# Perceiver mixer on one core: keys projected by weight columns of four strips and dealt on chip to stacked rows

## The chip, the core and the metric

One core of a Trainium2 chip runs the whole program in one launch. The metric is device time in microseconds from a timed run; lower is better. The kernel before was timed three times; a profiled execution was taken besides.

## What is computed

One block of a perceiver over 32 batches of 64 tokens of width 256: cross attention to 1601 context tokens per batch (16 heads of 16), a selective scan, and a mixture of 64 experts with top 8, each behind a layer norm and added to x. The change concerns the attention scores:

```python
q = _qdq(x) @ _qdq(wq).T + bq
kv = cond @ wkv.T + bkv
k, v = jnp.split(kv, 2, axis=-1)
...
attn = jax.nn.softmax(jnp.einsum('bnhd,bmhd->bhnm', q, k) * scale, axis=-1)
o = jnp.einsum('bhnm,bmhd->bnhd', attn, v).reshape(B, N, C)
```

## The kernel before

There are three phases: the mixer (attention, scan, routing), the experts, and a combining phase. The change touches the mixer alone. It works on 16 pairs of batches. A pair has 16 strips, called slots 0 to 15 of the pair: a strip is one batch, two heads by 64 queries (128 rows), against all 1604 padded keys. `step_of` (L371) turns a strip's number into batch `b`, half of the width `g` and place `s` among four. The 1604 keys lie in four chunks (`QUADS`) of 401 (`CK`).

Every engine runs the same loop over strips G. In TensorE's loop (L748) a strip does, in order: scores of G (`scores`, L616); transposes of the probabilities of strip G-1 (`turn`, L633), in two parts; one unit of the values of a coming batch (`v_mm`, L606; none in slots 0 and 8); the other transposes; the product of probabilities and values for four strips in flight (`times_v`, L643); keys for strip G+4 (`k_mm`, L594). Between them stand the small jobs of the table `MIX` (L58): the query product, output transposes, projections and routing of other pairs; slot 5 has `oqT` and `proj`, slot 8 has `XQ` ahead of the keys and `Q` behind them.

The keys of one strip are 32 rows wide. `k_mm` multiplies 32 weight columns by the four chunks and puts chunk c on PSUM partitions 32c to 32c+31, so four products of 32 columns stand side by side in TensorE. ScalarE (`k_up`, L780) writes the rounded high part `K_hi` from PSUM with the bias, VectorE (`k_low`, L959) the remainder `K_lo`; both are in the reduced fp32r format. `scores` then forms hi x hi, hi x lo and lo x hi, each as four products of 32 rows in the four row tiles, added up in the four banks of `S`. The queries are split the same way on GpSimd (`part_q`, L489) and copied by SP (`deal_queries`, L394) to all four groups of 32 partitions, eight transfers per half pair.

PSUM has one tile `S` of four banks, a ring of three banks for keys, values, transposes and small jobs in the order of the list `JOBS` (L131), and `O`. A job takes the bank of the job three places earlier when ScalarE (transposes) or VectorE (all others) has freed it (`take`, L559). VectorE takes the maximum of S over 1604 columns (`strip_max`, L976), ScalarE the exponential (`soft`, L796).

SP issues all transfers but the scatters, in the program order of its own loop (L418): query deals in slots 0 and 12, one zeroing transfer per strip in the first 48 strips (`clear`, `clear_y`), x rows, the next contexts in slots 4 and 11 (`load_ctx`), and, in slot 6 of a pair with a mixer turn, the row matrix B and C out to memory and, after waiting for it, back as `BC` to all partitions (L441 to L447).

## Time and profile before

| | us |
|---|---|
| timed runs, median of three (lowest, highest) | 2299.77 (2297.57, 2302.56) |
| profiled execution, first to last instruction (span) | 2296.0 |
| TensorE (PE) busy | 2102.5 (92%) |
| VectorE (DVE) busy | 1751.3 (76%) |
| ScalarE (ACT) busy | 1441.0 (63%) |
| GpSimd (POOL) busy | 684.0 (30%) |

The record of the profiled execution has its span; what lies around the span is seen only in the timed runs, whose median is 3.8 us longer. TensorE's products are pipelined: each record lasts longer than the step from one to the next, so the work of a block is read from the start of one block to the start of the next, not from busy time. A line of the time listing merges neighbouring records of one line and shape; a record count of twice the products means fp32, which takes two passes. A line of busy time by stretch holds the window, its us, a comma, the busy us (and records) of PE, PEld, DVE, ACT and POOL, then the granted clock (PEclk), the mean busy share of the 16 DMA engines, which may pass 1 by overlap at the edges, and GB/s.

### The profile page before, as it was taken

Reading aid. Unit: us, or ns where it says so; the run is one execution under the profiler, and the core shown is the slowest. Engines: PE = TensorE matmul, PEld = TensorE weight load, DVE = VectorE, ACT = ScalarE, POOL = GpSimd, SP = SyncE. Lnnn points to the kernel's source line nnn. Section 1 sums busy time; section 2 is a strip of 40 time slices with the busy share of each in tenths; the row PEclk is TensorE's granted clock in tenths of the full one; section 3 lists DMA queues with packets and bytes.
Section 4 is the critical chain, followed back from the end, with each engine's and each line's share of the span. In section 5 each row is a group of like instructions: output and inputs, shape, how many; then the busy total and the mean of one; then the engine's idle time right before and its main releaser. Section 6 shows DMA issues by size and latency. Waiting matters only on the chain. (4 is left out here: it accounts for less than half of the span.)

```text
span 2296.0 us, 56054 instructions
## 1 busy us (share of the span) xinstructions
PE 2102.5 (92%) x21448; PEld 1456.2 (63%) x21448; DVE 1751.3 (76%) x3728; ACT 1441.0 (63%) x3012; POOL 684.0 (30%) x646
## 2 busy tenths in 40 slices
PE   7999999999999999999999999999997149999975
PEld 5666666666666666666666666666664037777754
DVE  5557887979797978888888888797978736656646
ACT  2667676768676767676777767676867124444433
POOL 1002040404131322213130404040403427767770
PEclk9999999999999999999999999999999569999998
DMA  7586672323132313232323323232310136676648
GB/s 226 192 288 210 235 250 75 114 82 89 72 89 72 93 70 91 77 83 79 100 88 82 97 64 105 55 105 68 107 47 25 56 119 212 199 229 209 201 138 331
DMA packets 132711, 294.16 MB, mean 128 GB/s; under 512 B 21899, under 2 KB 89143, under 8 KB 126304
## 3 DMA queue, kind: packets, MB, share of 16 engines
q1 hardware_dynamic: 114016, 255.89, 35.7%
q0 software_dynamic: 18432, 34.69, 4.3%
q8 instruction: 174, 2.85, 0.5%
q14 instruction: 89, 0.73, 0.1%
HBM read 165.40 MB, written 108.27 MB: 119 GB/s over the span
## 5 line engine op out<-in xcount | busy, mean ns | idle before, releaser
L801 ACT ACTIVATE sb_probs<-S,sb_negmax 128x1604 f32<-128x1604 f32 x256 | 409.2, 1598 | 278.5 <-DVE sb_negmax L979 277.0
L793 ACT ACTIVATE sb_probsT<-W 128x384 f32<-128x384 f32 (+1 forms) x1024 | 473.6, 513 | 68.2 <-PE W L639 65.3
L639 PE MATMUL W<-sb_ident,sb_probs 128*128 128x128 f32 (+1 forms) x3328 | 478.3, 280 | 15.7 <-DVE sb_o_tok L992 8.0
L979 DVE TENSOR_REDUCE sb_negmax<-S 128x1 f32<-128x1604 f32 x256 | 466.2, 1821 | 2.9 <-PE S L629 1.2
L639 PEld LDWEIGHTS W<-sb_ident,sb_probs 128*128 128x128 f32 (+1 forms) x3328 | 363.5, 139 | 133.9 <-issue 64.7
L612 PE MATMUL W<-sb_wkv_in,sb_ctx 128*128 128x256 f32 (+1 forms) x1664 | 410.7, 389 | 14.2 <-ACT sb_probsT L793 6.6
L602 PE MATMUL W<-sb_ctx,sb_wkv_in 128*32 128x401 f32 x4096 | 399.3, 504 | 4.4 <-DVE sb_V L973 2.9
L612 PEld LDWEIGHTS W<-sb_wkv_in,sb_ctx 128*128 128x128 f32 (+1 forms) x1664 | 293.3, 187 | 79.1 <-ACT sb_probsT L793 25.7
L1335 POOL DMA_INDIRECT y_scratch<-sb_ys,sb_places x256 | 264.4, 1033 | 112.1 <-issue 109.0
L963 DVE SCALAR_TENSOR_TENSOR sb_K_lo<-W,sb_pair_cols,sb_K_hi 128x401 fp32r<-128x401 f32 x256 | 162.2, 633 | 175.5 <-ACT sb_K_hi L785 175.2
L785 ACT ACTIVATE sb_K_hi<-W,sb_pair_cols 128x401 fp32r<-128x401 f32 x256 | 153.2, 598 | 181.5 <-PE W L602 181.4
L512 POOL TENSOR_TENSOR sb_bx<-sb_u,sb_BC 128x512 f32<-128x512 f32 x128 | 164.9, 1305 | 340.9 <-DVE sb_u L1105 219.3
L657 PE MATMUL O<-sb_probsT,sb_V 128*32 128x128 f32 (+1 forms) x6656 | 245.0, 277 | 0.0
L602 PEld LDWEIGHTS W<-sb_ctx,sb_wkv_in 128*32 128x32 f32 x4096 | 129.2, 110 | 120.5 <-issue 104.1
L657 PEld LDWEIGHTS O<-sb_probsT,sb_V 128*32 128x32 f32 (+1 forms) x6656 | 173.9, 110 | 48.1 <-issue 39.5
L524 POOL DMA_INDIRECT xe_scratch<-sb_row,sb_sc_idx x128 | 156.2, 1221 | 43.8 <-issue 31.0
L973 DVE COPY sb_V<-W 128x512 f32<-128x512 f32 (+1 forms) x224 | 144.9, 647 | 26.1 <-PE W L612 25.1
L629 PEld LDWEIGHTS S<-sb_K_hi,sb_Q_hi 32*128 32x128 f32 x1024 | 49.8, 182 | 161.4 <-issue 158.9
L540 POOL TENSOR_TENSOR sb_st<-sb_st,sb_neg_half 128x1 f32<-128x1 f32 x16 | 8.8, 548 | 422.7 <-DVE sb_st L1086 422.7
L1456 DVE TENSOR_TENSOR sb_hid<-U,sb_sg 96x512 f32<-96x512 f32 x64 | 44.0, 687 | 112.5 <-PE U L1364 111.6
L535 POOL TENSOR_TENSOR sb_st<-sb_st,sb_neg_half 128x1 f32<-128x1 f32 x16 | 9.1, 566 | 397.3 <-DVE sb_st L893 397.3
L629 PE MATMUL S<-sb_K_hi,sb_Q_hi 32*128 32x400 f32 (+1 forms) x1024 | 116.5, 444 | 11.4 <-ACT sb_probs L801 9.3
(188 smaller groups left out, 2921.0 us busy)
## 6 DMA issues: line engine op xcount, KB each, us to landing
sb_ctx<-ctxT SPq DMA_DIRECT2D x32, 1604.0 KB, 7.7
xe_scratch<-sb_none SPq DMA_DIRECT2D x32, 1088.0 KB, 12.7
sb_xg<-xe_scratch SPq DMA_DIRECT2D x64, 544.0 KB
sb_BC<-bc_scratch SPq DMA_DIRECT2D x32, 1024.0 KB, 5.9
sb_Q_hi<-sb_q_hi SPq DMA_DIRECT2D x128, 128.0 KB, 4.5
sb_Q_lo<-sb_q_lo SPq DMA_DIRECT2D x128, 128.0 KB, 5.4
y_scratch<-sb_none SPq DMA_DIRECT2D x16, 1024.0 KB, 12.0
sb_rows<-y_scratch SPq DMA_DIRECT2D x16, 1024.0 KB, 8.1
```

The source lines that it names most:

```text
L512: pool.tensor_tensor(bx[:, mine, :], u[:, h, :].unsqueeze(1).to_broadcast([P, QS, P]), BC[:, mine, :], ALU.mult).then_inc(pool_up, 1)
L524: pool.indirect_dma_start(dram["xe"], bass.IndirectOffsetOnAxis(ap=sc_idx[:, t:t + 1], axis=0), row3[:], None, bounds_check=E * CAP - 1, o ...
L602: ins = pe.matmul(W[32 * c:32 * c + 32, 0:CK], wkv_in[:, k, w0:w0 + 32], ctx_t[b][:, k, c * CK:(c + 1) * CK], start=(k == 0), stop=(k == D ...
L612: ins = pe.matmul(W[0:keys_in(t), n * D:(n + 1) * D], ctx_t[b][:, k, t * P:t * P + keys_in(t)], wkv_in[:, k, D:2 * D], start=(k == 0), sto ...
L629: ins = pe.matmul(S[:, 512 * c:512 * c + cn], q[half][rows, s, g, :, :].rearrange("p h n -> p (h n)"), k[rows, s, 0:cn], start=(n == 0), s ...
L639: ins = pe.transpose(W[0:keys_in(t), at * P:(at + 1) * P], probs[n % 2][:, t * P:t * P + keys_in(t)], ident[:])
L657: ins = pe.matmul(O[32 * s:32 * s + 32, 0:P], V[b][0:keys_in(t), t, g * P + 32 * s:g * P + 32 * s + 32], probsT[k][n % (k + 1)][0:keys_in( ...
L793: act.activation(probsT[k][n % (k + 1)][:, 0:wide], ring[bank_of("T", G, k)][:, 0:wide], ACT.Copy)\
L801: act.activation(probs[n % 2][:].rearrange("p (c k) -> p c k", c=QUADS), scores_of, ACT.Exp, bias=negmax[:, slot:slot + 1], accum_out=den[ ...
L963: dve.scalar_tensor_tensor(K_lo[:, s, 0:CK], bank("K", n)[:, 0:CK], pair_cols[:, g * STRIPS + s:g * STRIPS + s + 1], K_hi[:, s, 0:CK].bitc ...
L979: dve.tensor_reduce(negmax[:, slot:slot + 1], scores_of, AX.XY, ALU.max, negate=True).then_inc(max_done, 1)
L1335: pool.indirect_dma_start(dram["y"], bass.IndirectOffsetOnAxis(ap=places[e % 4][:, c:c + 1], axis=0), ys[n][:, c, :], None, bounds_check=T ...
```

## The change

The weight columns of four strips (a full 128) are multiplied by one chunk at a time, so one key job now gives chunk c for four strips, and four jobs give all chunks. `K_hi` and `K_lo` hold 128 rows (four strips by 32) and are doubled. SP deals each strip's 32 rows to a tile `K_of` as hi, lo, hi on rows 0 to 95 (three transfers per strip, `deal_keys`), and the queries to `Q_of` as hi, hi, lo. Scores are then one product of 96 rows for each chunk. Key jobs run six strips ahead (`LEAD`), not four; the zeroing transfers are spread over more strips. The bias is a column per half, not per strip.

```diff
+CLEAR_AT = {n + n // 4: n for n in range(CLEARS)}
+Y_CLEAR_AT = {48 + 4 * n: n for n in range(Y_CLEARS)}
...
+
+LEAD = 6
...
     turns = [("T", G, k) for k in range(STRIPS)] if 0 < G <= ALL_STRIPS else []
...
-    keys = [("K", G + STRIPS)] if G + STRIPS < ALL_STRIPS else []
+    keys = [("K", G + LEAD)] if G + LEAD < ALL_STRIPS else []
...
-START = [("K", 0), ("K", 1), ("XQ", 0), ("K", 2), ("Q", 0), ("K", 3)]
+START = [("K", 0), ("K", 1), ("XQ", 0), ("K", 2), ("Q", 0), ("K", 3), ("K", 4), ("K", 5)]
...
         + [job for G in range(END) for job in jobs_at(G)])
...
-        K_hi, K_lo = (sb(f"K_{m}", [P, STRIPS, CK + 1], F32R) for m in ("hi", "lo"))
+        K_hi, K_lo = ([sb(f"K_{m}{n}", [P, QUADS, CK + 1], F32R) for n in range(2)] for m in ("hi", "lo"))
+        K_of = [sb(f"K_of{n}", [P, QUADS, CK + 1], F32R) for n in range(2)]
...
-        Q_hi, Q_lo = ([sb(f"Q_{m}{n}", [P, STRIPS, 2, 2, N], F32R) for n in range(2)] for m in ("hi", "lo"))
+        Q_of = [sb(f"Q_of{n}", [P, STRIPS, 2, 2, N], F32R) for n in range(2)]
...
         probsT = [[sb(f"probsT{k}{n}", [P, WIDTHS[0] * P]) for n in range(k + 1)] for k in range(STRIPS)]
...
+        k_in = [sem(f"k_in{n}") for n in range(2)]
...
-            (q_cols[:], io["bq"]), (pair_cols[:], io["bk"]),
+            (q_cols[:], io["bq"]), (k_cols[:], io["bk"]),
...
                 sp.wait_ge(q_up, pair + 1)
                 after(sp, s_done, pair * SLOTS - SLOTS // 2 * (1 - half))
-                for part, whole in ((q_hi, Q_hi), (q_lo, Q_lo)):
-                    for c in range(QUADS):
-                        sp.dma_start(whole[half][32 * c:32 * c + 32, :, :, :, :].rearrange("p s g h n -> p s (g h n)").bitcast(F32),
-                                     part[:, 2 * half:2 * half + 2, :, :].rearrange("p g h n -> p (g h n)").bitcast(F32)).then_inc(q_in[half], 16)
+                for at, part in enumerate((q_hi, q_hi, q_lo)):
+                    sp.dma_start(Q_of[half][32 * at:32 * at + 32, :, :, :, :].rearrange("p s g h n -> p s (g h n)").bitcast(F32),
+                                 part[:, 2 * half:2 * half + 2, :, :].rearrange("p g h n -> p (g h n)").bitcast(F32)).then_inc(q_in[half], 16)
+
+            def deal_keys(n):
+
+                four, s = divmod(n, STRIPS)
+                sp.wait_ge(ring_free["dve"], free_at("K", four * QUADS + QUADS - 1))
+                after(sp, s_done, n - 1)
+                for at, part in enumerate((K_hi, K_lo, K_hi)):
+                    sp.dma_start(K_of[n % 2][32 * at:32 * at + 32, :, :].rearrange("p c k -> p (c k)").bitcast(F32),
+                                 part[four % 2][32 * s:32 * s + 32, :, :].rearrange("p c k -> p (c k)").bitcast(F32)).then_inc(k_in[n % 2], 16)
             def clear(n):
...
             deal_queries(0, 0)
+            deal_keys(0)
+            deal_keys(1)
             sp.wait_ge(none_up, 1)
             for G in range(END):
...
+                if G + 2 < ALL_STRIPS:
+                    deal_keys(G + 2)
                 if slot == 0 and cur:
                     deal_queries(i, 1)
                 if slot == 12 and nxt:
                     deal_queries(i + 1, 0)
-                if G < CLEARS:
-                    clear(G)
-                elif G < CLEARS + Y_CLEARS:
-                    clear_y(G - CLEARS)
+                if G in CLEAR_AT:
+                    clear(CLEAR_AT[G])
+                if G in Y_CLEAR_AT:
+                    clear_y(Y_CLEAR_AT[G])
                 if slot == 0 and nxt:
                     sp.wait_ge(ring_full, full_at("XQ", i))
...
                     after(sp, dve_up, dve_at(i - 2, "X2"))
...
                 if nxt and slot in (4, 11):
-                    sp.wait_ge(ring_full, full_at("K", G + STRIPS - (1 if slot == 4 else 0)))
+                    sp.wait_ge(ring_full, full_at("K", i * SLOTS + (7 if slot == 4 else 15)))
                     load_ctx(i + 1, slot // 8)
                 if m == 2 and p is not None:
                     sp.wait_ge(ring_free["dve"], free_at("xp", p))
...
-            for part in (K_hi, K_lo):
+            for part in (*K_hi, *K_lo):
...
-                    after(pool, q_in[half], 16 * 2 * QUADS * i)
+                    after(pool, q_in[half], 16 * 3 * i)
...
             def k_mm(n):
-                b, g, s = step_of(n)
+                b, g, c = step_of(n)
                 W = take("K", n)
                 pe.wait_ge(ctx_in[b], 16 * (n // SLOTS + 1))
-                w0 = g * P + 32 * s
                 for k in range(DT):
-                    for c in range(QUADS):
-                        ins = pe.matmul(W[32 * c:32 * c + 32, 0:CK], wkv_in[:, k, w0:w0 + 32],
-                                        ctx_t[b][:, k, c * CK:(c + 1) * CK], start=(k == 0), stop=(k == DT - 1))
+                    ins = pe.matmul(W[:, 0:CK], wkv_in[:, k, g * P:(g + 1) * P],
+                                    ctx_t[b][:, k, c * CK:(c + 1) * CK], start=(k == 0), stop=(k == DT - 1))
...
             def v_mm(pair, b, unit):
...
                 if s == 0 and g == 0:
-                    pe.wait_ge(q_in[half], 16 * 2 * QUADS * (n // SLOTS + 1))
-                pe.wait_ge(ring_free["dve"], free_at("K", n))
+                    pe.wait_ge(q_in[half], 16 * 3 * (n // SLOTS + 1))
+                pe.wait_ge(k_in[n % 2], 16 * 3 * (n // 2 + 1))
                 after(pe, exp_done, n)
-                products = ((Q_hi, K_hi), (Q_hi, K_lo), (Q_lo, K_hi))
-                for n, (q, k) in enumerate(products):
-                    for c in range(QUADS):
-                        rows = slice(32 * c, 32 * c + 32)
-                        cn = CK + 1 if c == 0 else CK - 1
-                        ins = pe.matmul(S[:, 512 * c:512 * c + cn], q[half][rows, s, g, :, :].rearrange("p h n -> p (h n)"),
-                                        k[rows, s, 0:cn], start=(n == 0), stop=(n == len(products) - 1))
+                for c in range(QUADS):
+                    cn = CK + 1 if c == 0 else CK - 1
+                    ins = pe.matmul(S[:, 512 * c:512 * c + cn], Q_of[half][0:96, s, g, :, :].rearrange("p h n -> p (h n)"),
+                                    K_of[n % 2][0:96, c, 0:cn], start=True, stop=True)
                 ins.then_inc(s_done, 1)
             def turn(G, k):
...
-                if G + STRIPS < ALL_STRIPS:
-                    k_mm(G + STRIPS)
+                if G + LEAD < ALL_STRIPS:
+                    k_mm(G + LEAD)
...
             def k_up(n):
-                _, g, s = step_of(n)
+                _, g, c = step_of(n)
+                four = n // QUADS
                 act.wait_ge(ring_full, full_at("K", n))
-                after(act, s_done, n - STRIPS + 1)
-                act.activation(K_hi[:, s, 0:CK], ring[bank_of("K", n)][:, 0:CK], ACT.Identity,
-                               bias=pair_cols[:, g * STRIPS + s:g * STRIPS + s + 1]).then_inc(k_hi_up, 1)
+                if c == 0:
+                    for half in range(2):
+                        after(act, k_in[half], 16 * 3 * 2 * (four - 1))
+                act.activation(K_hi[four % 2][:, c, 0:CK], ring[bank_of("K", n)][:, 0:CK], ACT.Identity,
+                               bias=k_cols[:, g:g + 1]).then_inc(k_hi_up, 1)
             def turned(G, k):
...
-            for n in range(STRIPS):
+            for n in range(LEAD):
...
-                if G + STRIPS < ALL_STRIPS:
-                    k_up(G + STRIPS)
+                if G + LEAD < ALL_STRIPS:
+                    k_up(G + LEAD)
...
             def k_low(n):
-                _, g, s = step_of(n)
+                _, g, c = step_of(n)
+                four = n // QUADS
                 dve.wait_ge(k_hi_up, n + 1)
-                dve.scalar_tensor_tensor(K_lo[:, s, 0:CK], bank("K", n)[:, 0:CK],
-                                         pair_cols[:, g * STRIPS + s:g * STRIPS + s + 1],
-                                         K_hi[:, s, 0:CK].bitcast(F32), ALU.add, ALU.subtract).then_inc(ring_free["dve"], 1)
+                dve.scalar_tensor_tensor(K_lo[four % 2][:, c, 0:CK], bank("K", n)[:, 0:CK], k_cols[:, g:g + 1],
+                                         K_hi[four % 2][:, c, 0:CK].bitcast(F32), ALU.add, ALU.subtract).then_inc(ring_free["dve"], 1)
             def v_up(pair, b, unit):
...
                 if slot == 6 and i >= 2:
...
-                if G + STRIPS < ALL_STRIPS:
-                    k_low(G + STRIPS)
+                if G + LEAD < ALL_STRIPS:
+                    k_low(G + LEAD)
                 if slot == 8 and nxt:
...
     def cols(v):
...
-    def pair_cols(v):
-        return np.tile(v.reshape(DT * STRIPS, 2 * DH).T, (QUADS, 1))
-
...
-        "bk": pair_cols(a["L0_xattn_bkv"][:D]), "bv": a["L0_xattn_bkv"][D:],
+        "bk": cols(a["L0_xattn_bkv"][:D]), "bv": a["L0_xattn_bkv"][D:],
```

## Rows read from the trace of the kernel before

**Rows 1.** Busy time by stretch, the mixer's; columns as told above.
```profile
33.00:1760.00 1727.00, 1671.95 (x19226) 1132.68 (x19230) 1408.74 (x2889) 1223.32 (x2559) 378.84 (x335) 1.00 0.35 110
```

**Rows 2.** Busy time by stretch, three strips: slots 5, 13 and 15.
```profile
932.07:940.39 8.32, 7.84 (x83) 5.33 (x79) 5.91 (x14) 4.17 (x8) 0.55 (x1) 1.00 0.01 2
...
987.38:994.26 6.88, 6.45 (x78) 4.45 (x74) 6.32 (x11) 5.36 (x13) 1.65 (x2) 1.00 0.95 199
...
1000.87:1007.09 6.22, 6.22 (x78) 4.44 (x74) 5.73 (x9) 5.44 (x12) 0.00 (x0) 1.00 0.48 107
```

**Rows 3.** PE in order of time, slot 15: start, us, engine, line, operation.
```profile
1000.87 0.45 PE L629 MATMUL S<-sb_K_hi,sb_Q_hi 32*128 32x402 f32 x4
1001.15 0.35 PE L629 MATMUL S<-sb_K_lo,sb_Q_hi 32*128 32x402 f32 x4
1001.34 0.35 PE L629 MATMUL S<-sb_K_hi,sb_Q_lo 32*128 32x402 f32 x4
1001.62 0.98 PE L639 MATMUL W<-sb_ident,sb_probs 128*128 128x128 f32 x7
1002.44 1.92 PE L612 MATMUL W<-sb_wkv_in,sb_ctx 128*128 128x256 f32 x8
1004.20 0.82 PE L639 MATMUL W<-sb_ident,sb_probs 128*128 128x128 f32 x6
1004.95 0.86 PE L657 MATMUL O<-sb_probsT,sb_V 128*32 128x128 f32 x24
1005.62 1.53 PE L602 MATMUL W<-sb_ctx,sb_wkv_in 128*32 128x401 f32 x16
1007.09 0.46 PE L629 MATMUL S<-sb_K_hi,sb_Q_hi 32*128 32x402 f32 x4
```

**Rows 4.** PE in order of time, slot 8 from probabilities times values on.
```profile
956.75 1.08 PE L657 MATMUL O<-sb_probsT,sb_V 128*32 128x128 f32 x32
957.76 0.44 PE L581 MATMUL W<-sb_ident,sb_x_q 128*128 128x128 f32 x2
...
959.61 1.16 PE L590 MATMUL W<-sb_xqT,sb_wqT 128*128 128x128 f32 x8
960.70 0.45 PE L629 MATMUL S<-sb_K_hi,sb_Q_hi 32*128 32x402 f32 x4
```

**Rows 5.** PE and DVE in order of time in the experts' phase, one expert.
```profile
1998.86 1.04 PE L1353 MATMUL XT<-sb_ident,sb_xg 128*128 128x128 f32 x8
...
1999.73 1.89 PE L1375 MATMUL Y<-sb_wd,sb_hid 96*128 96x256 f32 x8
2000.13 1.28 DVE L1430 TENSOR_TENSOR sb_x_lo<-XT,sb_x_hi 128x512 fp32r<-128x512 f32 x2
...
2001.52 0.68 PE L1364 MATMUL G<-sb_x_hi,sb_w_hi 128*96 128x512 f32 x2
```

**Rows 6.** PE and DVE in order of time, slot 5 and the start of slot 6.
```profile
937.19 1.13 PE L685 MATMUL W<-sb_wpT,sb_oqT 128*128 128x256 f32 x4 [0.48 <-DVE sb_V L973]
...
938.25 0.86 PE L657 MATMUL O<-sb_probsT,sb_V 128*32 128x128 f32 x24
...
941.17 0.64 DVE L963 SCALAR_TENSOR_TENSOR sb_K_lo<-W,sb_pair_cols,sb_K_hi 128x401 fp32r<-128x401 f32 x1 [0.34 <-ACT sb_K_hi L785]
```

**Rows 7.** Busy time by stretch: query deals, deals crowded, BC, early, later.
```profile
1003.00:1004.00 1.00, 1.00 (x7) 0.87 (x6) 1.00 (x1) 1.00 (x3) 0.00 (x0) 1.00 0.71 237
...
988.00:990.00 2.00, 1.57 (x17) 1.16 (x10) 1.93 (x5) 2.00 (x8) 1.09 (x1) 1.00 1.16 190
950.00:954.00 4.00, 4.00 (x53) 2.71 (x51) 3.45 (x8) 3.15 (x6) 0.00 (x0) 1.00 1.02 422
33.00:140.00 107.00, 103.35 (x1192) 71.37 (x1192) 53.50 (x69) 69.23 (x127) 3.88 (x4) 0.98 0.69 240
...
900.00:1000.00 100.00, 97.07 (x1118) 65.84 (x1121) 83.53 (x181) 70.06 (x147) 26.17 (x23) 1.00 0.26 81
```

**Rows 8.** SP's queue in order of time: the two BC loads of one pair.
```profile
948.28 0.81 SPq L446 DMA_DIRECT2D sb_BC<-bc_scratch  x2
```

More of the change, by code:

```diff
@@ L230, in mixer_phase @@
         q_cols = sb("q_cols", [P, DT])
-        pair_cols = sb("pair_cols", [P, DT * STRIPS])
+        k_cols = sb("k_cols", [P, DT])
         bv_row = sb("bv_row", [P, D])
@@ L470, in _ @@
                       allow_small_or_imprecise_dtypes=True).then_inc(consts, 1)
-            pool.wait_ge(consts, 9)
+            pool.wait_ge(consts, 11)
             pool.affine_select(out=ident[:], in_=ident[:], compare_op=ALU.not_equal, fill=1.0, base=0,
@@ L478, in _ @@
                                pattern=[[1, P]], channel_multiplier=-1).then_inc(consts, 1)
-            pool.wait_ge(consts, 12)
+            pool.wait_ge(consts, 14)
             pool.affine_select(out=headmask[:], in_=headmask[:], compare_op=ALU.is_ge, fill=0.0, base=DH * STRIPS - 1,
                                pattern=[[DH * STRIPS, 2]], channel_multiplier=-1).then_inc(consts, 1)
-            pool.wait_ge(consts, 13)
+            pool.wait_ge(consts, 15)
             def rstd_q(i):
@@ L564, in take @@
                 return ring[bank_of(*job)]
-            pe.wait_ge(consts, 13)
+            pe.wait_ge(consts, 15)
             def turn_w(rows, bank, parts):
```

## Prediction

> **What bounds the kernel now.** I read the stretches first, then the strips of one pair, then TensorE's blocks inside a strip, then the places where TensorE waits, then the DMA share. The mixer takes 1727 us of the 2296.0 us span; PE is busy 1672 us of it at granted clock 1.00, the 2.4 GHz level [rows 1]. Every step of the diff lies in this stretch. 256 strips in 1727 us are 6.75 us each. A strip with no extra work (slot 15 of a pair) takes 6.22 us, all PE [rows 2], and its blocks add up to that with nothing over: scores 0.75, seven transposes 0.82, values 1.76, six transposes 0.75, probs times values 0.67, keys 1.47 [rows 3]. So there PE's own time is the strip. Not everywhere: slot 13 has the same jobs and takes 6.88, and slot 5 takes 8.32 [rows 2], where proj adds 1.06 [rows 6] and oqT, two transposes and the way into the next block, some 0.4: 7.7. The rest is waiting on a bank that VectorE has not freed. In slot 5 proj waits for the copy of V, and K_lo then waits for K_hi, made from this strip's keys [rows 6]: a loop through both engines. By the same subtraction slots 1 to 6, 10, 13 and 14 hold 0.5 us or more of waiting; 0, 7, 9, 11, 12 and 15 are PE's; 8 is discussed below. So a price on PE must be taken apart by where in the strip it falls.
>
> **Keys.** Before: eight products of 32 weight columns per strip, four at a time in the four column tiles. After: two products of 128 columns per strip, each two passes of 401 columns. The values block is such work: 8 passes of 256 columns in 1.76 us are 0.22 each [rows 3], so 401 columns are 0.34, and four passes 1.35 or so. The old block is 1.47, that is also four rounds of 0.34, plus 0.02 of stagger and about 0.09 until the scores may start. The column tiles were already full; full weight columns gain nothing by themselves.
>
> **Scores.** Before: three products (hi hi, hi lo, lo hi), each four row tiles at once, a steady step of 0.19 (1001.15 to 1001.34; both ends are rounded, I use 0.18) [rows 3]. After: one product over 96 rows, four chunks one after another: four passes, not three, 4 x 0.18 = 0.73. So the stacking adds a pass of 0.18.
>
> **Changes of tile shape.** What can pay for that pass is what PE loses each time the tile shape changes. Leaving row tiles: the last step is 0.28, not 0.19, and the seven transposes take 0.82, which is 0.06 over 7 x 0.109 (0.109 is the step of the eight in [rows 5]). Entering them: the first step is 0.28, 0.10 over the steady one, after the 0.09 at the end of keys [rows 3]. Together 0.34 per strip, gone if 96 rows run as the full array. They seem to: eight 128-row transposes take 0.87, 8 x 0.109 with nothing added, though the next products have 96 rows; the 0.06 at their other end comes with a VectorE result that ended at 2001.41, 0.1 before PE went on, so it is a wait [rows 5]. But a new change appears, from probs times values (column tiles, unchanged) to full-width keys, which used to share the shape. Its price is in slot 8: 32 records of probs times values take 1.01 before a full transpose, against 0.67 x 32/24 = 0.89, so 0.12; and the eight passes of the query product, between column tiles and row tiles, take 1.09 where steps of 0.11 give 0.89; 0.09 of the rest is the exit, 0.10 a first weight load that could not run ahead [rows 4]. Entry to full-width keys: 0.22.
>
> The Trainium skill, "TensorEngine Tiling (Array Packing)", Key Properties, says that a change of tiling mode drains the engine, and its list of modes has 128, 64 and 32 rows, none of 96. By it the 96 rows either cost nothing or, if they were a mode, would keep the drains; the rows here show no price.
>
> **Sum for a strip that is PE's own**, from the end of probs times values to the second transpose. Before: 1.47 + 0.75 + 0.06 = 2.28. After: 0.22 + 1.35 + 0.73 = 2.30. Net +0.02 (bounds: -0.20 if the entry price stays hidden, +0.13 if the change from plain fp32 products to fp32r ones costs 0.11, as [rows 5] could also be read: 0.06 ahead of the first and as much in a first weight load that did not run ahead).
>
> **Strips with a loop through VectorE.** There the 0.34 saved lies around the scores, where PE waits for a bank anyway, while the 0.22 lies ahead of keys, in the loop keys, K_hi, K_lo, maximum, V copy. So from 0 (VectorE alone sets the pace) to +0.22 (the loop of slot 5 [rows 6]); slot 13 waits without an added PE block, so neither end holds for all nine, and I take +0.11.
>
> **Slot 8** runs XQ ahead of keys and Q behind them, both full: two changes fewer there, 0.5 us less PE, but VectorE is busy with routing; I count -0.2 (0 to -0.5).
>
> Per pair: six at +0.02, slot 8 at -0.2, nine at +0.11: +0.9 us; 16 pairs +14 us (bounds -5 and +34).
>
> **ScalarE and VectorE.** k_up and k_low keep count, shape and place; only the bias column differs. k_up's new wait, once per four strips, is for deals issued two strips before: free. LEAD 6 puts two key blocks (2.9 us of PE) into the start and takes them from the last strips; at the start PE waits for VectorE, so I take 0 (bounds -3 to +3). Four memsets instead of two on POOL run during the weight loads: nothing.
>
> **Deals.** New: per strip three transfers of 32 x 6432 bytes, 617 KB. No such transfer is in the trace; the nearest is the query deal, also onto 32 partitions: 237 GB/s when it starts, 190 GB/s at full DMA share with several in flight [rows 7]. So 2.6 to 3.3 us per strip of 6.75; I take 3. Query deals fall from 16 to 6 per pair and give back about 7 us per pair. Later in the mixer the share is 0.26 [rows 7]: 26 + 45 - 7 = 64 of 109 us, no bound. Early, with the clears, it is 0.69 of 107 us [rows 7]: 74 + 42 to 53 - 7 - 8 (three clears fewer in 16 strips) = 101 to 112 of 107. That can just saturate: 0 to 5 us per pair for two and a half pairs, I take 4 us in all (bounds 0 to 20).
>
> The Trainium skill, "SBUF — State Buffer", Door 1, speaks against this part: 32 partitions reach 8 of 16 ports, 189 GB/s at 1 MiB, and two transfers do not add up; estimate by it 3.3 us per strip, the slow end of the rows.
>
> SP now waits in every strip for the scores two strips ahead of use, and all that it issues later queues behind that: contexts, BC, x. A deal issued after the scores of G must land before those of G+2, 12 to 14 us later; issue is about 2 us and transfer 3. The tightest is slot 9's: BC's 2 MB are issued at 948.28 [rows 8], move at 422 GB/s [rows 7], are through near 954, the deal takes till about 957 and lands near 959; the scores were at 960.70 [rows 4]. One us to spare: hidden, but barely.
>
> **Forecast.** 2296.0 + 14 + 4 = 2314 us of span. The median of the runs, 2299.77, lies 3.8 above the profiled span; so 2318 us.
>
> **Rivals.**
> *The entry to full-width keys is hidden* (faster). The weight load of the first key pass runs ahead under probs times values. For: ordinary full-to-full changes cost 0. Against: [rows 4] price it after the same block. Then -0.20 in six strips, about -0.1 in nine, slot 8 -0.3: -2.4 per pair, -38 us, half of it eaten by VectorE's loops: about 2283. It decides as soon as the measured entry is under about 0.1 us.
> *All is absorbed* (same). The mixed strips take 0 and the early DMA holds: 2296 + 2 + 0 to 4, 2303 on the median.
> *The scores pay at their entry* (slower). 0.11 in each strip, +27 us, less a third absorbed: 2336.
> *Deals land late* (slower). If BC and the deal together need 3 us more than reckoned, slot 9 is 2 us late per pair, +32 us: 2350. It shows as PE waiting for a DMA at the scores.
> *No full columns in effect*: the products are what the diff says, so I give this nothing.
>
> **Chances.** Forecast (2308 to 2328) 0.42; hidden entry 0.16; absorbed 0.18; scores pay 0.13; late deals 0.11. The range 2292 to 2350 leaves out the hidden entry and the far end of late deals. A measurement of this kernel can tell about 0.2% (2295.2 to 2304.4) from no change: faster 0.16, within 0.20, slower 0.64.
>
> **What would show it.** Keys start to scores start near 1.45, scores start to first transpose near 0.73, probs times values 0.12 longer: right. Scores with a first step well over 0.18: 96 rows do pay. Key blocks without a longer first pass: hidden entry. PE idle at the scores with a DMA as releaser: late deals. DMA share of 33 to 250 us at 0.95 or more with longer strips only there: the clears collide. The prediction is wrong if the strip of slot 15 moves by more than 0.1 us either way, or if the strips with waiting do not grow.

## Result and the profile after

The kernel after takes 2323.22 us (median of four runs, 2321.43 to 2324.79), the kernel before on the same chip 2298.96 (2297.57 to 2302.56): ratio 1.0104, 95% interval 1.0092 to 1.0116. It is slower by 1.0%, as forecast (2318, range 2292 to 2350). The sum of the span, by stretches between the first scores of the pairs in TensorE's time listing:

| stretch | before, us | after, us | forecast | measured |
|---|---|---|---|---|
| start to the first scores | 33.40 | 37.21 | 0 | +3.8 |
| pairs 0 to 2 | 317.19 | 327.84 | +2.7 and +4 | +10.65 |
| pairs 3 to 14 | 1313.05 | 1324.71 | +10.8 | +11.66 |
| pair 15, to its last scores | 96.13 | 93.67 | +0.9 | -2.5 |
| behind that | 536.2 | 538.5 | 0 | +2.3 |
| span | 2296.0 | 2321.9 | +18.4 | +25.9 |

Three lines of the page of after: PE's busy time, DMA shares in 40 slices, and SP's queue (packets, MB, share of 16 engines). The transfers went from 294.16 to 430.68 MB in all.
```profile
PE 2119.4 (91%) x16328; PEld 1593.0 (69%) x16328; DVE 1752.0 (75%) x3728; ACT 1444.9 (62%) x3012; POOL 677.4 (29%) x648
...
DMA  6999976767677766566666657565745136666648
...
q1 hardware_dynamic: 127840, 393.02, 61.5%
```
Busy time by stretch of after, columns as in [rows 1]: the mixer; slots 5, 13 and 15 of pair 8, answering [rows 2]; pair 1 and pair 2 with the clears, then a later stretch, answering [rows 7].
```profile
37.20:1784.05 1746.85, 1683.33 (x14153) 1264.38 (x14154) 1408.19 (x2886) 1226.23 (x2559) 369.15 (x335) 1.00 0.70 187
...
951.48:959.95 8.47, 7.88 (x62) 5.86 (x60) 6.08 (x14) 4.17 (x8) 0.36 (x1) 1.00 0.64 208
1007.47:1014.35 6.88, 6.49 (x55) 4.98 (x54) 6.36 (x10) 5.62 (x14) 1.86 (x2) 1.00 0.81 201
1020.96:1027.30 6.34, 6.34 (x55) 4.95 (x54) 5.79 (x9) 5.44 (x12) 0.00 (x0) 1.00 0.46 99
...
140.69:250.04 109.35, 105.11 (x893) 79.39 (x891) 79.90 (x138) 76.98 (x160) 14.45 (x13) 1.00 0.94 285
250.04:365.05 115.01, 108.62 (x902) 81.66 (x901) 92.64 (x195) 78.11 (x164) 25.38 (x23) 0.99 0.78 220
...
900.00:1000.00 100.00, 96.91 (x825) 72.57 (x824) 82.52 (x180) 68.72 (x142) 18.64 (x19) 1.00 0.60 149
```
Slot 15 went from 6.22 to 6.34, slot 5 from 8.32 to 8.47, slot 13 stayed at 6.88; the DMA share is 0.94 in pair 1 and 0.60 later (0.26 before). PE in order of time in slot 15, answering [rows 3] (start, us, line, operation):
```profile
1020.96 1.20 PE L642 MATMUL S<-sb_K_of,sb_Q_of 96*128 96x402 f32 x4
1021.99 0.93 PE L652 MATMUL W<-sb_ident,sb_probs 128*128 128x128 f32 x7
1022.79 1.99 PE L628 MATMUL W<-sb_wkv_in,sb_ctx 128*128 128x256 f32 x8
1024.62 0.82 PE L652 MATMUL W<-sb_ident,sb_probs 128*128 128x128 f32 x6
1025.37 0.87 PE L670 MATMUL O<-sb_probsT,sb_V 128*32 128x128 f32 x24
1026.16 1.61 PE L618 MATMUL W<-sb_ctx,sb_wkv_in 128*128 128x401 f32 x4
1027.30 0.66 PE L642 MATMUL S<-sb_K_of,sb_Q_of 96*128 96x402 f32 x1
```
From start to start: scores 1.03, transposes 0.80, values 1.83, transposes 0.75, probs times values 0.79, keys 1.14. The scores' first record now begins while the last key pass still runs, so keys and scores are read together: 2.17. Of the entry to full-width keys, 0.12 shows as the longer block ahead of them (0.79 against 0.67), 0.10 as the first key pass (0.44; the others take 0.34).

A steady pair (the sum of the medians over pairs 2 to 14, slot by slot) takes 110.37 us against 109.35: +1.01. Single slots go from -0.24 (slot 1) and -0.20 (slot 4) to +0.21 (slot 0) and +0.34 (slot 3); slots 11, 13 and 14 stand still.

### The profile page after: what moved, and what is told of

It is laid out like the page before. It is cut to its first block and busy times, and to the rows that moved or that the text cites. A ratio compares the mean times of both kernels' runs of the same rounds, so it can differ in the third digit from the quotient of the medians.

```text
span 2321.9 us, 46485 instructions
## 1 busy us (share of the span) xinstructions
PE 2119.4 (91%) x16328; PEld 1593.0 (69%) x16328; DVE 1752.0 (75%) x3728; ACT 1444.9 (62%) x3012; POOL 677.4 (29%) x648
## 2 busy tenths in 40 slices
DMA packets 146500, 430.68 MB, mean 185 GB/s; under 512 B 31627, under 2 KB 78391, under 8 KB 140128
## 5 line engine op out<-in xcount | busy, mean ns | idle before, releaser
L652 PE MATMUL W<-sb_ident,sb_probs 128*128 128x128 f32 (+1 forms) x3328 | 466.4, 276 | 17.2 <-DVE sb_o_tok L1008 5.9
L652 PEld LDWEIGHTS W<-sb_ident,sb_probs 128*128 128x128 f32 (+1 forms) x3328 | 385.6, 139 | 79.4 <-DVE sb_o_tok L1008 16.7
L618 PE MATMUL W<-sb_ctx,sb_wkv_in 128*128 128x401 f32 x1024 | 413.4, 527 | 4.8 <-DVE sb_V L989 2.6
L642 PE MATMUL S<-sb_K_of,sb_Q_of 96*128 96x400 f32 (+1 forms) x1024 | 296.8, 412 | 16.3 <-ACT sb_probs L817 9.4
L980 DVE SCALAR_TENSOR_TENSOR sb_K_lo<-W,sb_k_cols,sb_K_hi 128x401 fp32r<-128x401 f32 x256 | 162.1, 633 | 194.4 <-ACT sb_K_hi L801 193.9
L801 ACT ACTIVATE sb_K_hi<-W,sb_k_cols 128x401 fp32r<-128x401 f32 x256 | 152.9, 597 | 208.4 <-PE W L618 205.1
L618 PEld LDWEIGHTS W<-sb_ctx,sb_wkv_in 128*128 128x128 f32 x1024 | 175.0, 190 | 129.7 <-issue 39.8
L642 PEld LDWEIGHTS S<-sb_K_of,sb_Q_of 96*128 96x128 f32 x1024 | 188.6, 191 | 85.8 <-issue 23.7
L542 POOL DMA_INDIRECT xe_scratch<-sb_row,sb_sc_idx x128 | 147.7, 1154 | 43.9 <-issue 31.1
```

Source lines behind the costliest of these rows:

```text
L618: ins = pe.matmul(W[:, 0:CK], wkv_in[:, k, g * P:(g + 1) * P], ctx_t[b][:, k, c * CK:(c + 1) * CK], start=(k == 0), stop=(k == DT - 1))
L642: ins = pe.matmul(S[:, 512 * c:512 * c + cn], Q_of[half][0:96, s, g, :, :].rearrange("p h n -> p (h n)"), K_of[n % 2][0:96, c, 0:cn], star ...
L652: ins = pe.transpose(W[0:keys_in(t), at * P:(at + 1) * P], probs[n % 2][:, t * P:t * P + keys_in(t)], ident[:])
L801: act.activation(K_hi[four % 2][:, c, 0:CK], ring[bank_of("K", n)][:, 0:CK], ACT.Identity, bias=k_cols[:, g:g + 1]).then_inc(k_hi_up, 1)
L980: dve.scalar_tensor_tensor(K_lo[four % 2][:, c, 0:CK], bank("K", n)[:, 0:CK], k_cols[:, g:g + 1], K_hi[four % 2][:, c, 0:CK].bitcast(F32), ...
```

## The two parts taken apart

The first three kernels are the kernel before with the keys alone, the scores alone, or both, and no transfers. Without the deals the scores multiply rows that are not the right ones; the work has the same shapes.

**Keys alone**, in the kernel before:
```diff
-                    for c in range(QUADS):
-                        ins = pe.matmul(W[32 * c:32 * c + 32, 0:CK], wkv_in[:, k, w0:w0 + 32],
-                                        ctx_t[b][:, k, c * CK:(c + 1) * CK], start=(k == 0), stop=(k == DT - 1))
+                    ins = pe.matmul(W[:, 0:CK], wkv_in[:, k, g * P:(g + 1) * P],
+                                    ctx_t[b][:, k, s * CK:(s + 1) * CK], start=(k == 0), stop=(k == DT - 1))
```


> The kernel before with one part of the change: keys by full weight columns (two products of 128 columns), everything else as before. It leaves out the dealing, so the rows of K hold other strips' keys and the scores are of the wrong keys. Theory (tile changes set the price): a new change of shape ahead of the keys, none gone around the scores; slot 15 of a pair goes from 6.22 to about 6.42 us, first key pass 0.44 with later ones 0.34, all runs near 2340 (2325 to 2350). Rival (full columns are cheaper by themselves, or the entry is hidden): slot 15 at or under 6.22, 2300 or less. Rival (the slowdown of the whole change comes from the transfers): no change, 2299.

Measured: 2323.18 us (2321.10 to 2323.69), ratio 1.0103 (1.0086 to 1.0120); slot 15 takes 6.39, a steady pair 110.7. PE in order of time, from probs times values of slot 15 to the scores:
```profile
1016.83 0.87 PE L655 MATMUL O<-sb_probsT,sb_V 128*32 128x128 f32 x24
1017.62 1.61 PE L600 MATMUL W<-sb_ctx,sb_wkv_in 128*128 128x401 f32 x4
1019.17 0.46 PE L627 MATMUL S<-sb_K_hi,sb_Q_hi 32*128 32x402 f32 x4
```
Keys take 1.55 to the scores and probs times values 0.79: 2.34, where [rows 3] has 0.67 + 1.47 = 2.14. The full columns cost 0.20 here and gain nothing; 0.03 of it is given back at the values, which no longer wait. 25 us in all, about as much as the whole change; the time lies 2 us under its range (2325 to 2350).

**Scores alone**, in the kernel before:
```diff
-                products = ((Q_hi, K_hi), (Q_hi, K_lo), (Q_lo, K_hi))
...
+                for c in range(QUADS):
+                    cn = CK + 1 if c == 0 else CK - 1
+                    ins = pe.matmul(S[:, 512 * c:512 * c + cn], Q_hi[half][0:96, s, g, :, :].rearrange("p h n -> p (h n)"),
+                                    K_hi[0:96, s, 0:cn], start=True, stop=True)
```


> The kernel before with the other part: scores as one product of 96 rows in four chunks, keys in column tiles as before. It leaves out the dealing and the low parts, so the products are taken of rows that lie there. Theory: a pass more (+0.18), no drain behind the scores (-0.14): slot 15 at 6.24 to 6.28, all runs 2298 to 2312. Rival (stacking saves time by itself): 2285 or less. Rival (an entry price for 96 rows of its own, 0.1 or more): slot 15 at 6.35 or more, 2320 or more.

Measured: 2299.23 us (2296.40 to 2302.30), ratio 1.0005 (0.9996 to 1.0015); slot 15 takes 6.22, a steady pair 109.3. PE in order of time, slot 15:
```profile
1000.63 1.00 PE L626 MATMUL S<-sb_K_hi,sb_Q_hi 96*128 96x402 f32 x4
1001.46 0.93 PE L636 MATMUL W<-sb_ident,sb_probs 128*128 128x128 f32 x7
1002.23 1.89 PE L612 MATMUL W<-sb_wkv_in,sb_ctx 128*128 128x256 f32 x8
```
Scores 0.83 for 0.75, transposes 0.77 for 0.82, values 1.72 for 1.76: four passes over 96 rows cost what three products in four row tiles and their way out cost.

**Both, no transfers**: the two edits together.

> Both parts together on the kernel before, without the transfers of keys and with keys four strips ahead as before; scores are of the wrong rows. Theory: here the change of shape between keys and scores goes too, so it is not the sum of the two parts: slot 15 at 6.35 as in the changed kernel, early pairs without their extra 7 us and the start without its 3.8: 2312 (2307 to 2317). Rival (transfers cause the slowdown): 2299 or less. Rival (parts add up): over 2340.

Measured: 2315.28 us (2314.66 to 2318.95), ratio 1.0070 (1.0053 to 1.0087); slot 15 takes 6.35, a steady pair 110.4. So the stacked product gives back 8 of the 25 us that full-width keys cost, the rest of the slowdown without transfers is +17 us, and the last 8 come with the transfers, the longer lead and the respread clears; the lead was not run by itself.

## The wait that the sum of slot 15 missed

PE's own sum was +0.02 for slot 15, the trace shows +0.13. In after the values block starts only when VectorE has made `K_lo` and so freed its bank. ScalarE and VectorE in order of time, slot 15 of before, then of after:
```profile
1001.01 0.60 ACT L785 ACTIVATE sb_K_hi<-W,sb_pair_cols 128x401 fp32r<-128x401 f32 x1 [0.80 <-PE W L602]
...
1001.68 0.63 DVE L963 SCALAR_TENSOR_TENSOR sb_K_lo<-W,sb_pair_cols,sb_K_hi 128x401 fp32r<-128x401 f32 x1
```
```profile
1021.47 0.60 ACT L801 ACTIVATE sb_K_hi<-W,sb_k_cols 128x401 fp32r<-128x401 f32 x1 [0.96 <-PE W L618]
...
1022.10 0.64 DVE L980 SCALAR_TENSOR_TENSOR sb_K_lo<-W,sb_k_cols,sb_K_hi 128x401 fp32r<-128x401 f32 x1
```
`K_lo` ends at 1002.31 in before and at 1022.74 in after. The first pass of the values takes 0.249 and 0.320 us, so the second starts at 1002.69 and 1023.11, in both 0.37 to 0.38 behind the end of `K_lo`: both wait for it, before by 0.03 (a pass is 0.218), after by 0.10, with another 0.03 in the last of the transposes. What changed is PE's way there: from `K_hi`'s start to the values 1.43 us in before, 1.32 in after. Not only the nine strips with a visible loop, this one too had no time to spare.

**Bank freed by ScalarE**, in the kernel after: `K_hi`'s completion frees the bank, and VectorE makes `K_lo` from SBUF.
```diff
-    return "act" if job[0] == "T" else "dve"
+    return "act" if job[0] in ("T", "K") else "dve"
...
-                               bias=k_cols[:, g:g + 1]).then_inc(k_hi_up, 1)
+                               bias=k_cols[:, g:g + 1]).then_inc(ring_free["act"], 1)
...
-                dve.scalar_tensor_tensor(K_lo[four % 2][:, c, 0:CK], bank("K", n)[:, 0:CK], k_cols[:, g:g + 1],
+                dve.scalar_tensor_tensor(K_lo[four % 2][:, c, 0:CK], K_hi[four % 2][:, c, 0:CK].bitcast(F32), k_cols[:, g:g + 1],
```


> The changed kernel with the PSUM bank of the keys freed by ScalarE as soon as K_hi is written; K_lo is computed by VectorE from K_hi in SBUF with the same size, so the low part is left out of the result. Theory (what the changed kernel saves around the scores it gives back at the values block, which waits for the bank that K_lo frees): the values block starts without its wait, slot 15 goes from 6.35 to about 6.25, and the whole by 10 to 25 us, to 2298 to 2313. Rival (the longer strip comes from TensorE's own steps alone): slot 15 stays at 6.35 and the whole within 5 us of 2323.

Measured: 2316.46 us (2314.99 to 2319.12), ratio 1.0074 (1.0057 to 1.0091). PE in order of time, slot 15:
```profile
1015.84 1.20 PE L643 MATMUL S<-sb_K_of,sb_Q_of 96*128 96x402 f32 x4
1016.87 0.93 PE L653 MATMUL W<-sb_ident,sb_probs 128*128 128x128 f32 x7
1017.64 1.89 PE L629 MATMUL W<-sb_wkv_in,sb_ctx 128*128 128x256 f32 x8
1019.37 0.82 PE L653 MATMUL W<-sb_ident,sb_probs 128*128 128x128 f32 x6
```
Transposes 0.77, values 1.73: the wait is gone and slot 15 takes 6.21. The time missed its range (2298 to 2313): the steady pair fell by 0.16 us only, since slot 13 gained 0.73 (6.88 to 6.15) and slot 14 lost 0.48 (6.61 to 7.09), and slot 9 lost as much (6.42 to 6.90).

**The same in the kernel before**:

> The kernel before, with the keys' bank freed by ScalarE after K_hi; VectorE makes K_lo from K_hi in SBUF, so the low part is not the true remainder. Theory (the values block waits for K_lo only in the kernel after, because its keys and scores are together 0.04 us shorter than the work of ScalarE and VectorE beside them): slot 15 can lose only the 0.03 us by which its first pass of values (0.249) is over 0.218, so 6.19; the pair loses 0 to 0.4 us, 2293 to 2299 us in all. Rival (the wait lies in every kernel alike and moving the bank is a gain of its own): slot 15 loses 0.13 us as it did in the kernel after, 6.09, and the time is 2292 us or less.

Measured: 2297.01 us (2295.83 to 2302.76), ratio 0.9992 (0.9983 to 1.0001); slot 15 takes 6.20, a steady pair 109.31. The theory's numbers. PE in order of time, slot 15:
```profile
1002.18 0.99 PE L639 MATMUL W<-sb_ident,sb_probs 128*128 128x128 f32 x7
1003.00 1.89 PE L612 MATMUL W<-sb_wkv_in,sb_ctx 128*128 128x256 f32 x8
1004.73 0.82 PE L639 MATMUL W<-sb_ident,sb_probs 128*128 128x128 f32 x6
```
The values take 1.73 here too. Where neither kernel waits for `K_lo`, slot 15 is 6.20 and 6.21: PE's own net is +0.01 where the sum had +0.02, and 0.11 is the wait. In the pair this wait is the smaller part. With the bank freed by ScalarE in both kernels a steady pair still differs by 0.90 us (110.21 against 109.31): slots 7, 12 and 15 then stand at +0.05, 0.00 and +0.01, but slot 0 keeps its +0.20, and slots 2, 3, 5, 6 and 10 keep +0.12 to +0.34.

**No low part**, in both: `K_lo` is filled with zeros once and VectorE's step left out.

> The kernel before without VectorE's part of the keys: K_lo is zero for good, the bank is freed by ScalarE, the products stay as they are. To be read against the next one. Theory (what the change adds to a steady pair goes through K_lo, the bank that it frees and VectorE; PE's own sum is level, 6.22 against 6.21): without K_lo the steady pairs of the two kernels differ by at most 0.3 us, and this one takes 2230 to 2285 us. Rival (PE's entry to full-width keys is paid in the strips with a loop whatever VectorE does): the pairs still differ by 0.9 us or more.

> The kernel after without VectorE's part of the keys: K_lo is zero for good, the bank is freed by ScalarE, the transfers stay, the clears are moved out of strips 20 to 24. Theory: a steady pair within 0.3 us of that of the kernel before without K_lo, and the time within 5 us of it (the start is 3 to 4 us longer and the last pair as much shorter). Rival: the pair is longer by 0.9 us or more and the time by 14 us or more.

Measured: 2231.87 us (2229.33 to 2233.67) and 2255.01 (2251.64 to 2262.99), each against 2300.33 of before on that chip: ratios 0.9705 (0.9692 to 0.9718) and 0.9818 (0.9801 to 0.9835). The steady pairs are 105.02 and 105.71: +0.70, more than the theory's 0.3, less than the rival's 0.9. So, by subtraction, 0.32 of the 1.01 us goes through VectorE's `K_lo`, and 0.70 does not. That part lies in slots 0, 10 and 14 (+0.15 to +0.16 each) and 6 (+0.10); nine strips, slot 15 among them, stand at +0.02 to +0.04; slots 3, 4 and 9 at +0.23, -0.20 and -0.18. PE in order of time in slot 14, scores and the values, of the first kernel and then of the second:
```profile
750.04 0.45 PE L628 MATMUL S<-sb_K_hi,sb_Q_hi 32*128 32x402 f32 x4
...
752.22 1.08 PE L611 MATMUL W<-sb_wkv_in,sb_ctx 128*68 128x256 f32 x4 [0.45 <-ACT sb_probsT L792]
```
```profile
760.17 1.20 PE L645 MATMUL S<-sb_K_of,sb_Q_of 96*128 96x402 f32 x4
...
762.71 1.08 PE L631 MATMUL W<-sb_wkv_in,sb_ctx 128*68 128x256 f32 x4 [0.57 <-ACT sb_probsT L812]
```
In slot 14 it is the same thing with another engine: the values wait for a bank that ScalarE frees, 0.57 us instead of 0.45. That what is saved around the scores (0.34 us less the added pass of 0.18) goes into this wait, which is 0.12 longer, while the 0.22 paid ahead of the keys stays, is what the two records suggest; no run takes ScalarE's copies away, and for slots 0, 3, 6 and 10 the cause is open. The medians of the runs differ by 23 us, not by 16 times 0.70: in the second kernel pairs 0 to 2 take 314.6 us against 307.7, and PE waits for dealt keys in later pairs too (slot 8 of pair 11: 8.40 against 6.53). With strips 0.3 us shorter some of the deals no longer land in time.

## Where the keys stand in the strip

**Keys ahead of probs times values**, in the kernel after and in the kernel before. Keys then follow transposes, which are full-width too.
```diff
-                    if in_flight(G):
-                        times_v(G)
...
-                    if in_flight(G):
-                        times_v(G)
                 if G + LEAD < ALL_STRIPS:
                     k_mm(G + LEAD)
+                if in_flight(G):
+                    times_v(G)
```


> The changed kernel with the keys block moved ahead of probabilities times values in each strip; same work, same result. The number of changes of shape stays. Theory (loops through VectorE run over the keys, and the values block waits for K_lo): K_lo comes 0.7 us earlier, the wait at the values block goes, strips that wait on VectorE get shorter; against it keys wait for the bank that the copy of V frees, 0.2 us in ordinary strips. 2290 to 2312. Rival (the wait for the bank of V takes all of it): 2320 or more.

> The kernel before with the same move alone. Theory: the loops through VectorE get shorter by up to 0.5 us in the nine slots that wait: 2265 to 2295. Rival: keys wait for the bank of V: 2300 or more.

Measured: 2331.93 us (2330.50 to 2355.58), ratio 1.0176 (1.0121 to 1.0231), and 2295.45 (2292.34 to 2298.94), ratio 0.9986 (0.9977 to 0.9996): the rival's time in the first, just over the theory's range in the second. PE in order of time, slot 15 of the first:
```profile
1026.59 0.82 PE L652 MATMUL W<-sb_ident,sb_probs 128*128 128x128 f32 x6
1027.54 1.61 PE L618 MATMUL W<-sb_ctx,sb_wkv_in 128*128 128x401 f32 x4
1029.08 0.86 PE L670 MATMUL O<-sb_probsT,sb_V 128*32 128x128 f32 x24
1029.88 0.45 PE L642 MATMUL S<-sb_K_of,sb_Q_of 96*128 96x402 f32 x1
```
The transposes take 0.95 until the keys instead of 0.75: keys now wait for VectorE's copy of V, which frees their bank. And the price of the changed shape has only moved: keys 1.54, probs times values 0.80, and the scores' first pass 0.29. One block in column tiles costs one way in and one way out in both places. In before the move gained 0.60 in slot 13 and 0.53 in slot 2, lost 0.65 in slot 1 and 0.20 in slot 15, and the pair fell by 0.37 (109.35 to 108.98): the one kernel that leaves out no work and whose interval lies below before's time, by 0.14%.

**The same in slots 12 and 13 alone**, of the kernel before:

> The kernel before, with the block of keys ahead of probs times values in slots 12 and 13 of every pair only. Theory (the order pays where the transposes or proj behind it wait for K_lo, and costs 0.2 us where keys then wait for the copy of V; with it everywhere, slots 13 and 14 lost 0.60 and 0.09 us, slot 12 gained 0.08): slot 13 at 6.28 instead of 6.88, slots 14 and 15 at 6.5 to 6.6 and 6.22, the steady pair 108.7 to 108.9, 2288 to 2293 us. Rival (VectorE's sequence sets the pace here, and what slot 13 gains is handed back in slots 14 and 15, as it was with the bank freed by ScalarE): the pair stays at 109.2 to 109.4, 2296 to 2301 us.

Measured: 2300.60 us (2296.08 to 2304.02), ratio 1.0005 (0.9996 to 1.0014), a steady pair 109.41, the rival's numbers: slot 13 fell to 6.28 as expected, but slot 12 rose from 6.56 to 7.31, for the keys stood there 0.67 us for the copy of V. PE's record of it:
```profile
766.50 1.55 PE L603 MATMUL W<-sb_ctx,sb_wkv_in 128*32 128x401 f32 x16 [0.67 <-DVE sb_V L976]
```
What one strip gains here a neighbour loses, but not the neighbours that the rival named: slots 14 and 15 take 6.52 and 6.22, and the loss lies in slot 12, in the wait that the theory had put at 0.2 us.

## The transfers

One strip's deal in after, a time without other loads, by busy time in stretches of 1 us (last column GB/s):
```profile
1023.00:1024.00 1.00, 1.00 (x6) 0.87 (x6) 1.00 (x1) 1.00 (x3) 0.00 (x0) 1.00 0.86 188
1024.00:1025.00 1.00, 1.00 (x8) 0.87 (x7) 0.65 (x2) 1.00 (x3) 0.00 (x0) 1.00 1.00 212
1025.00:1026.00 1.00, 1.00 (x28) 0.77 (x26) 0.96 (x3) 1.00 (x2) 0.00 (x0) 1.00 0.95 193
1026.00:1027.00 1.00, 1.00 (x13) 0.55 (x4) 0.97 (x2) 0.95 (x4) 0.00 (x0) 1.00 0.14 32
```
About 3.1 us for 617 KB, as taken. The Trainium skill, "SBUF — State Buffer", Door 1, has 189 GB/s for 32 partitions at 1 MiB, from which the estimate was 3.3 us; the rows, 188 to 212 GB/s with three transfers in flight, agree to within an eighth. In a steady pair the deals cost nothing that shows: slot by slot, after and the kernel with both parts and no transfers agree to 0.03 us in the median. Early they cost. The scores' line over the whole run (idle before it, weight loads and products counted each: us, times):
```profile
  DMA sb_K_of<-sb_K_hi: 13.6, 12
```
PE and, below it, SP's queue, in pair 2:
```profile
317.16 1.00 PE L642 MATMUL S<-sb_K_of,sb_Q_of 96*128 96x402 f32 x4 [3.13 <-DMA sb_K_of<-sb_K_hi]
```
```profile
296.74 0.87 SPq L420 DMA_DIRECT2D xe_scratch<-sb_none  x1
299.35 0.34 SPq L459 DMA_DIRECT2D bc_scratch<-sb_BCT  x1
304.50 0.81 SPq L464 DMA_DIRECT2D sb_BC<-bc_scratch  x2
305.41 0.51 SPq L414 DMA_DIRECT2D sb_K_of<-sb_K_hi  x1
```
SP waits for BC to be in memory before it asks for it back: 5.15 us here, with a clear issued just ahead (2.04 us in pair 8: 966.17 to 968.21). The deal queues behind that on SP, then shares the DMA engines with BC's 2 MB, and the scores of slot 9 wait 3.13 us. Behind that wait the granted clock fell. Busy time by stretch, in the wait and behind it:
```profile
313.00:317.00 4.00, 1.02 (x8) 0.83 (x8) 3.37 (x11) 1.18 (x4) 1.70 (x3) 1.00 0.98 210
...
319.00:321.00 2.00, 2.00 (x7) 1.64 (x6) 1.03 (x1) 1.85 (x5) 1.41 (x2) 0.50 0.90 197
```
PE was busy for 1.02 of 4 us, then the clock stood at 0.50, the 1.2 GHz level, and slot 9 took 7.70 us instead of its usual 6.42: this late deal costs 1.28 us on top of its wait.

**Clears kept out of strips 20 to 24**, in the kernel after:
```diff
-CLEAR_AT = {n + n // 4: n for n in range(CLEARS)}
+QUIET = [G for G in range(37) if not 20 <= G <= 24]
+CLEAR_AT = {G: n for n, G in enumerate(QUIET)}
```


> The changed kernel with the 32 zeroing transfers of xe issued in strips 0 to 19 and 25 to 36, so that none lies in slots 4 to 8 of the second pair or next to the contexts and BC of the third. Theory (early deals are late because they queue behind clears, contexts and BC): slots 8 and 9 of pairs 1 and 2 lose their 6 us, the whole goes to 2315 to 2319. Rival (the early excess has another cause): within 2 us of 2323.

Measured: 2315.59 us (2315.17 to 2317.15), ratio 1.0072 (1.0055 to 1.0089): 7.6 us back, so that by the medians nothing is left of what the transfers had cost against the kernel without them (2315.28). Pairs 0 to 2 take 322.3 us (after 327.8, no transfers 320.2), so 2.1 us are left there. Slots 8 and 9 of pairs 1 and 2 are 5.9 us shorter together, as the theory has it, and slot 2 of the same pairs is 1.6 longer. Another 1.4 lie in slot 1 of pair 0 (9.04 in after, 7.66 here, 7.62 without transfers), where the granted clock stood at 0.50 for 6.8 us in after and for 3.4 in the other two, with no wait for a deal.

**Both edits**, the bank freed by ScalarE and the moved clears:

> The kernel after with both edits: the keys' bank freed by ScalarE (the low part is not the true remainder) and the clears moved out of strips 20 to 24. Theory (two costs in different places, 3 us of steady pairs and 8 us of early transfers): they add, 2309 to 2313 us, steady pair 110.17, early pairs 1 and 2 at 110 to 111. Rival (both edits gave back the same early transfers): 2314 to 2317 us.

Measured: 2317.40 us (2313.65 to 2320.22), ratio 1.0072 (1.0058 to 1.0086). The rival: they don't add. The steady pair is at 110.18, but slot 2 of pairs 1 and 2 takes 10.45 and 11.06 (8.74 and 8.65 with the clears moved alone). PE stood idle there for VectorE's `sb_o_tok` (1.92 and 1.41 us; 1.77 and 0.58 with the clears moved alone), and behind both waits the granted clock was at 0.50 for 3.4 us, which it was not with the clears moved alone. Why `sb_o_tok` comes late is left open.

## The prediction, step by step

- **PE's time is the strip in slot 15 "with nothing over"**: the step that failed. The values block of 1.76 in [rows 3] already held a wait of 0.03 (eight steps of 0.218 are 1.74, and without `K_lo` it takes 1.73), so the slack behind `K_lo` was nil. I placed the 0.34 saved ahead of a wait, and the 0.22 paid in the loop, for nine strips, and then counted the other strips by PE alone; the argument held for slots 7, 12 and 15 as well. Slot 15 moved by 0.13, over the 0.1 that I had named as the mark of an error. Slot 0, the largest of the six at +0.21, does not come from this wait (it keeps +0.20 with the bank freed early), and its cause is open.
- **Keys gain nothing, scores pay a pass, 96 rows run as the full array**: right. 2.17 for keys and scores against 0.10 + 1.35 + 0.73 = 2.18; in the trace with the bank freed early the transposes behind the scores take 7 times 0.11, with no way out to pay. The list of modes in the Trainium skill ("TensorEngine Tiling (Array Packing)", Available Configurations) has no 96 rows, and full-array cost here agrees with that. My mark "keys to scores 1.45, scores to transposes 0.73" was badly chosen: the first scores record starts before the last key pass ends, so the border shifts by 0.31 while the sum stands.
- **Entry to full-width keys 0.22**: right, 0.12 + 0.10. The rival that it stays hidden fell with that, and so did the scores that pay at their entry.
- **Slot 8 at -0.2**: wrong, +0.05. The drains are saved, and in pair 8 the query product then waits for a bank of ScalarE's copies (the keys ahead of it take 1.57, their last step 0.56 instead of 0.34).
- **Nine strips at +0.11**: over-sized, slots 1 to 6, 10, 13 and 14 give +0.50 together instead of +0.99. My second mark, that these strips grow, held for five of them (2, 3, 5, 6 and 10); 13 and 14 stood still, 1 and 4 got shorter. Slot 8 and the six strips of PE's own give +0.52 instead of -0.08. The two errors cancel: +1.01 a pair against +0.9. The total was right in part by luck.
- **Start and LEAD, net 0**: right as far as single profiles tell. Against the kernel without transfers and with keys four ahead, the start is 4.2 us longer (33.05 to 37.21) and the last pair 4.1 shorter (97.75 to 93.67); but the start alone lies between 32.95 and 35.38 in the kernels with keys four ahead.
- **Deals**: 3 us right. The later share was reckoned as 64 of 109 us, 0.59, but its 26 and 45 were those of a stretch of 100 us; over 109 us the same rates give 69, 0.63, and 0.60 was measured. From 33 to 250 us the share is 0.92, under the 0.95 that I had named as the mark of clears that collide; they did. Slot 9's deal "hidden but barely" right (in pair 8 its scores waited 0.24 us). Late deals, the rival, came true in one strip each of pairs 1 and 2 (1.44 and 3.13 us before the product) and for under 0.7 us in slot 9 of pairs 8, 14 and 15. The early collision has the right mechanism and the wrong size: pairs 0 to 2 take 7.65 us more than without transfers, 6.2 of it in pairs 1 and 2, against 4, inside its bounds. The fall of the clock behind a late deal was not in the sum.
- **Outside the mixer, nothing**: +2.3 in these two profiles, which no line of the diff explains, and which goes with the full-width keys: behind the last scores the profiles of the eight kernels that have them take 537.7 to 540.9 us, those of the six others 534.7 to 536.6. In after the clock fell for a while at the end of the stretch 200 to 300 us past the last scores; before, the whole of that stretch has 1.00 (97.66 of 100 us busy). Busy time by stretch of after:
```profile
2060.00:2070.00 10.00, 10.00 (x53) 7.75 (x52) 6.07 (x14) 4.08 (x8) 4.93 (x5) 1.00 0.77 240
...
2070.00:2083.00 13.00, 10.57 (x39) 7.20 (x38) 4.57 (x11) 4.05 (x8) 9.41 (x10) 0.74 0.85 292
```
  The mean of 0.74 says that part of those 13 us ran at the 1.2 GHz level, after PE had been busy throughout; what set it off is open. It is not the whole of the +2.3: four of the eight have 1.00 in that stretch, the kernel without transfers, with its 540.9 us, among them.
- **3.8 us between span and median**: too much. A run of after took 2323.66 with a span of 2321.9, so 1.8 lies around the span; the rest of the 3.8 was the spread of the runs, and it made up for a part of what the sum lacked.

## To carry to other kernels

Before counting a saving on the busiest engine, look at what the next block waits for: if the saved time lies between a producer and the release of its buffer, the wait grows by what was saved (in slot 15 the way is 0.11 us shorter, the wait 0.10 longer), and a block that took 0.03 us more than its steps was the only sign of it here. A saving or a price in one strip is not that of the next: the same edit moved single strips of a pair from -0.24 to +0.34 us. A change of tile shape has two prices, the way out of the old and the first weight load of the new, and which neighbours a block has decides them; widening the keys took them out of a shape that they shared with the block ahead. Transfers that are free in the steady state are to be costed again where a queue also holds a wait for another transfer, and a wait of the busiest engine can cost more than its length where the granted clock falls behind it.

## What was not expected of the hardware

One product over 96 rows in four passes takes as long as three products in four row tiles with their way out, both behind column tiles: 2299.23 against 2298.16 us for the kernel, 6.22 for the strip in both. Coming from column tiles, the first pass is 0.10 longer than the next whether it is the scores (0.29 against 0.18) or the full-width keys (0.44 against 0.34).
